# A Mamba and mixture-of-experts block on one core: scan inputs and products over pairs of steps, one table set for Exp and Ln, a wider dt projection, and new orders of the queues

## The chip, the cores and the metric

The kernel runs on 1 core of a Trainium2 chip, in float32 but for small helpers. The metric is the device time of one execution in microseconds. Before the change it is 13,945.11 us, the median of 3 runs (13,933.89 to 13,954.32).

## The reference

16 images of 224x224x3 become 196 patch tokens each, and with 128 text tokens they are 16 sequences (B = 16) of L = 324 tokens with 192 channels. They are normalised, pass 16 Mamba layers (NL = 16, inner width I = 384, state N = 16, rank 48), a final norm, and a mixture of 16 experts with a shared expert. The layers, where nearly all the time goes, compute for each sequence:

```python
h = rmsnorm(x, nw)
u, z = split(h @ in_w.T)
u = silu(causal_conv(u, cw, cb))                       # 4 taps
dt_r, Bm, Cm = split(u @ xp_w.T)                       # 48, 16, 16
dt = softplus(dt_r @ dtw.T + dtb)
for t in range(L):                                     # 16 states n for each of 384 channels i
    state = exp(dt[t, i] * A[i, n]) * state + dt[t, i] * u[t, i] * Bm[t, n]
    y[t, i] = sum_n state[i, n] * Cm[t, n]
x = x + ((y + u * D) * silu(z)) @ ow.T
```

## The kernel before

A *unit* is one sequence in one layer; there are UNITS = 256, layer after layer. All the work of the layers is in `run_layers`. Channels lie on partitions, time along the free axis, so one `tensor_tensor_scan` of VectorE runs a whole recurrence: its 972 elements are three blocks of 324 times. The 16 *steps* s of a unit cover 384 channels x 16 states; each step has 128 partitions (32 channels x 4 states) and 3 blocks, and has nothing to do with time. For each step:

- ScalarE makes the decay, three Exp activations of 323 elements (`se_decay`, L646), into one of two buffers in PSUM (`decay[s % 2]`), when the scan two steps before has left it. One column a block stays zero and cuts the recurrence.
- GpSimd makes the input, `dbu` = `dtu_rep` * `b_rep` (`ge_dbu`, L912), into one of DRING = 4 buffers.
- VectorE scans (`ve_scan`, L847) into one of RING = 8 buffers `h`, and multiplies by C in place (`ve_product`, L856), C being in PSUM, where TensorE broadcasts it for four steps at a time (`te_bcast`, L466). The products of steps 3, 7 and 12 are GpSimd's (`ge_product`, L920) with a C in SBUF (`c_rep`).
- TensorE adds up the four states of a channel with the matrix `fold`, two steps in one `te_sum` (L479), in PSUM (`y_ps`); `te_skip` adds u * D.

When all 16 steps are in `y_ps`, VectorE multiplies by silu(z) (`ve_gate`, L864), and TensorE projects back and adds x (`te_out`). The rest of a unit is prepared ahead. In one step function with number u the engines scan unit u and work on p = u + 1 (softplus, z), k = u + 2 (u, convolution, Silu, x projection, dt projection) and j = u + 3 (norm). All of TensorE's projections go through one PSUM bank, `pj`: ScalarE copies each result out before the next may be written, so `te_z` half 1 waits for `se_z` half 0, and so on. dt = max(x, 0) + ln(1 + exp(-|x|)) + a correction of what 1 + e lost in rounding: ScalarE makes the terms, and three DMAs of GpSimd's queue add them into `dt` (L936), which SP's queue stores in DRAM, and loads back replicated for the 128 partitions of each step (`dt_rep`, `dtu_rep`, 486 KB a piece; `b_rep`, `c_rep`, 162 KB).

Each engine's queue is written out by hand in `tensor_step`, `scalar_step`, `vector_step`, `gpsimd_step` and `sync_step`, and runs strictly in its order; semaphores (`reached`, `wait`) tie them. VectorE's order around a unit's start is: product 15 of the unit before, scans 0 and 1, product 0, the gate of the unit before, scan 2. TensorE's is: sum of squares, sum of steps 12 and 13, broadcast 0, z half 0, sum of steps 14 and 15, z half 1, out. ScalarE switches its activation tables four times a unit (L778, L782, L697, L705): to Ln, to Exp, to Silu, to Exp. Three shorter steps (`early`) run before the loop.

## Time and profile before

| | us |
|---|---|
| median of 3 runs | 13,945.11 |
| profiled execution, span from first to last instruction | 13,964.1 |
| VectorE busy | 12,892.4 (92%) |
| GpSimd busy | 12,631.1 (90%) |
| TensorE busy | 12,204.2 (87%) |
| ScalarE busy | 11,365.0 (81%) |

The profile is of an execution of its own; of it the trace gives the span. The embedding and the first norm take the first 200 us, the layers run to about 12,800, the router and the experts after that. Engines: PE is TensorE's matmuls, PEld its weight loads, DVE VectorE, ACT ScalarE, POOL GpSimd, SP the queue that issues most DMAs. An instruction's end may overlap the start of the next on its engine, so the time that one takes of its engine is read from start to start. "[0.48 <-ACT ps L646]" means that the engine stood idle for 0.48 us before, and that the ScalarE instruction of line 646 ended the wait. "x3" means that three instructions in a row are merged in a row.

### The profile page before, as it was taken

The numbers are of one execution on the slowest core, as the hardware profiler recorded it, in microseconds if no ns is written. First come the engines' busy times: TensorE is split into PE (matmuls) and PEld (weight loads), VectorE is DVE, ScalarE is ACT, GpSimd is POOL, SyncE is SP. The second block draws the span as 40 slices with busy tenths as digits, with TensorE's granted clock in tenths as the row PEclk, the third lists the DMA queues.
The fourth block names the chain that finished last, engine by engine and source line by source line (L and its number), as shares of the span: only waits on it lengthen the run. The fifth ranks groups of instructions, "written<-read, shape, count | busy, mean of one in ns | idle before, by whom it ended". The sixth has DMA issues, their size and how long they took to land. (4 is left out here: it accounts for less than half of the span.)

```text
span 13964.1 us, 203073 instructions
## 1 busy us (share of the span) xinstructions
PE 12204.2 (87%) x51466; PEld 6379.1 (46%) x51466; DVE 12892.4 (92%) x8757; ACT 11365.0 (81%) x21744; POOL 12631.1 (90%) x6352
## 2 busy tenths in 40 slices
PE   7888888888888888888888888888888888888898
PEld 4444444444444444444444444444444444444776
DVE  2999999999999999999999999999999999997533
ACT  4888888888888888888888888888888888887111
POOL 2999999999999999999999999999999999996033
PEclk8999999999999999999999999999999999999899
DMA  4555555555555555555555555555555555554122
GB/s 104 156 160 157 156 164 161 166 154 161 157 161 161 162 161 155 162 156 165 160 165 155 159 159 156 166 161 163 155 161 156 163 161 161 161 155 128 36 63 52
DMA packets 825576, 2086.15 MB, mean 149 GB/s; under 512 B 101243, under 2 KB 381308, under 8 KB 825336
## 3 DMA queue, kind: packets, MB, share of 16 engines
q1 hardware_dynamic: 693720, 1684.45, 36.0%
q0 software_dynamic: 130992, 399.73, 15.2%
q14 instruction: 114, 0.93, 0.0%
q10 hardware_dynamic: 720, 0.55, 0.0%
q8 instruction: 30, 0.49, 0.0%
HBM read 1414.20 MB, written 286.41 MB: 122 GB/s over the span
## 5 line engine op out<-in xcount | busy, mean ns | idle before, releaser
L912 POOL TENSOR_TENSOR dbu<-dtu_rep,b_rep 128x972 f32<-128x972 f32 x4096 | 9534.2, 2511 | 137.2 <-DVE h L847 109.5
L847 DVE TENSOR_TENSOR_SCAN h<-ps,dbu 128x972 f32<-128x972 f32 x4096 | 8723.4, 2166 | 207.8 <-ACT ps L646 207.8
L646 ACT ACTIVATE ps<-dt_rep,A_cur 128x323 f32<-128x323 f32 x12288 | 5842.5, 520 | 957.0 <-DVE h L847 950.5
L856 DVE TENSOR_TENSOR h<-h,ps 128x972 f32<-128x972 f32 x3329 | 3731.2, 1146 | 0.2 <-DVE ps L1206 0.2
L479 PE MATMUL ps<-h,fold 128*32 128x486 f32 x16400 | 3567.5, 577 | 90.1 <-DVE h L856 89.4
L920 POOL TENSOR_TENSOR h<-h,c_rep 128x972 f32<-128x972 f32 x769 | 1853.0, 2410 | 0.0
L557 PE MATMUL ps<-u_raw,w_cv 128*128 128x162 f32 (+7 forms) x8256 | 1801.5, 372 | 28.6 <-ACT u_raw L682 1.5
L479 PEld LDWEIGHTS ps<-h,fold 128*32 128x32 f32 x16400 | 784.9, 110 | 1961.1 <-issue 1731.1
L557 PEld LDWEIGHTS ps<-u_raw,w_cv 128*128 128x128 f32 x8256 | 1351.6, 190 | 509.4 <-ACT u_pre L689 159.5
L543 PE MATMUL ps<-x_norm,w_u 96*128 96x324 f32 (+1 forms) x4128 | 987.7, 383 | 65.1 <-ACT u_raw L682 55.9
L466 PE MATMUL ps<-c_rows,sel_c 16*128 16x324 f32 x2048 | 827.8, 484 | 209.1 <-DVE h L856 201.2
L508 PE MATMUL ps<-x_norm,w_z 96*128 96x324 f32 (+1 forms) x4112 | 983.5, 383 | 1.4 <-ACT rstd L715 0.7
L525 PE MATMUL ps<-y_gated,w_o 128*96 128x324 f32 x3084 | 925.9, 436 | 0.0
L543 PEld LDWEIGHTS ps<-x_norm,w_u 96*128 96x128 f32 x4128 | 665.7, 191 | 541.1 <-ACT u_raw L682 277.9
L586 PE MATMUL ps<-xp_rows,w_dt 49*128 49x162 f32 (+1 forms) x2064 | 562.1, 393 | 388.7 <-ACT dt L743 207.8
L577 PE MATMUL ps<-u_act,w_x 128*128 128x324 f32 x1548 | 490.2, 453 | 461.8 <-ACT u_act L697 454.8
L1854 POOL DMA_INDIRECT e_rows<-n_rows,e_ix x96 | 96.3, 1003 | 863.7 <-issue 472.8
L508 PEld LDWEIGHTS ps<-x_norm,w_z 96*128 96x128 f32 x4112 | 661.1, 190 | 447.0 <-issue 179.5
L466 PEld LDWEIGHTS ps<-c_rows,sel_c 16*128 16x128 f32 x2048 | 299.9, 183 | 834.6 <-DVE h L856 629.8
L586 PEld LDWEIGHTS ps<-xp_rows,w_dt 49*128 49x128 f32 x2064 | 321.0, 187 | 788.0 <-ACT dt L743 429.6
L523 PE MATMUL ps<-x_T,ident 96*96 x1028 | 401.9, 473 | 315.8 <-ACT z_pre L670 201.9
L525 PEld LDWEIGHTS ps<-y_gated,w_o 128*96 128x96 f32 x3084 | 504.5, 164 | 337.0
(186 smaller groups left out, 12885.8 us busy)
## 6 DMA issues: line engine op xcount, KB each, us to landing
dt_rep<-dt_rows SPq DMA_DIRECT2D x1028, 486.0 KB, 5.6
dtu_rep<-dtu_rows SPq DMA_DIRECT2D x1028, 486.0 KB, 4.8
b_rep<-b_rows SPq DMA_DIRECT2D x1028, 162.0 KB, 5.2
dt<-exp_x POOLq DMA_DIRECT2D x257, 486.0 KB, 5.1
dt<-dtu POOLq DMA_DIRECT2D x257, 486.0 KB, 4.4
dt<-u_pre POOLq DMA_DIRECT2D x257, 486.0 KB, 4.4
dt_rows<-dt SPq DMA_DIRECT2D x257, 486.0 KB, 2.6
dtu_rows<-dtu SPq DMA_DIRECT2D x257, 486.0 KB, 2.6
```

The source lines that it names most:

```text
L466: pe.matmul(c_ps, sel_c[64:80, q, :], c_rows[par][64:80, :], start=True, stop=True).then_inc(s_cbc, 1)
L479: mm = pe.matmul(y_ps[32 * r:32 * r + 32, half, :], fold[:, :], src[:, half * YW:(half + 1) * YW], start=(m in (0, 1)), stop=(m < 0))
L508: mm = pe.matmul(pj[:, lo:hi], w_z[:, c, it * 128:it * 128 + 128], x_norm[par][:, c, t:t + hi - lo], start=(c == 0), stop=(c == 1))
L525: mm = pe.matmul(pj[0:HC, 0:L], w_o[:, it, half * HC:(half + 1) * HC], y_gated[:, it, :], start=False, stop=(it == IT - 1))
L543: mm = pe.matmul(pj[:, lo:hi], w_u[:, c, it * 128:it * 128 + 128], x_norm[par][:, c, t:t + hi - lo], start=(c == 0), stop=(c == 1))
L557: mm = pe.matmul(pj[:, lo + skip:hi], w_cv[:, it * KC + KC - 1 - back, :], u_raw[:, it * L + t + skip - back:it * L + t + hi - lo - back], ...
L586: mm = pe.matmul(pj[:, lo:hi], w_dt[:, it * 128:it * 128 + 128], xp_rows[0:RB, t:t + hi - lo], start=True, stop=True)
L646: ins = act.activation(decay[s % 2][:, it * L + 1:(it + 1) * L], dt_rep[:, s % NR, it, 1:L], ACT.Exp, scale=A_cur[:, it * N + s:it * N + s ...
L847: dve.tensor_tensor_scan(h[s % RING][:, :, :].rearrange("p i t -> p (i t)"), decay[s % 2], dbu[s % DRING][:, :, :].rearrange("p i t -> p ( ...
L856: dve.tensor_tensor(h[s % RING][:, :, :], h[s % RING][:, :, :], c_ps.unsqueeze(1).broadcast_to([128, IT, L]), ALU.mult).then_inc(s_prod, 1)
L912: pool.tensor_tensor(dbu[s % DRING][:, :, :], dtu_rep[:, r, :, :], b_rep[:, q, :].unsqueeze(1).broadcast_to([128, IT, L]), ALU.mult).then_ ...
L920: pool.tensor_tensor(h[s % RING][:, :, :], h[s % RING][:, :, :], c_rep[:, at, :].unsqueeze(1).broadcast_to([128, IT, L]), ALU.mult).then_i ...
```

## The change

- GpSimd's input is made for two steps in one instruction of 1944 elements (eight a unit). VectorE's products of steps 0 and 1, 4 and 5, 8 and 9, 10 and 11, 14 and 15 are pairs too; those of 2, 6 and 13 stay alone, and 3, 7 and 12 stay GpSimd's. `dbu` and `h` become one tensor each, so that neighbours lie side by side.
- The scans, Exps, products and sums run in lists of their own (`SCANS`, `EXPS`, `PRODUCTS`, `SUMS`), and the counts that others wait for follow these lists.
- Exp and Ln are taken from the set `natural_log_exp_and_others`; table switches stay only around Silu. What Ln gives at one in that set, measured on the chip at the start (`less`), is subtracted by one more pass over exp_x.
- The dt projection contracts all 128 rows of `xp_rows` with a `w_dt` padded by zeros, instead of 49 rows.
- All five queues have a new order. A step now ends in the middle of a unit: with number u it does the second part of unit u's scan and the first part of unit u + 1's (`v[0]`, `v[1]`), the convolution, dt and z of u + 2, the projection to u of u + 3, the norm of u + 4. Four early steps come before the loop. The gate of unit u stands after scans 1 and 0 of unit u + 1 and waits for the last sum of `SUMS`, that of steps 12 and 13.
- The memsets of `h`, `z_act`, `y_gated`, `c_rep`, `c_ps` and `y_ps` before the layers are gone, and the loop's last step needs no tail of products and outs behind it.

The diff, cut to its core (of the old step functions, which the listing above shows, nothing is repeated):

```diff
-MAIN_SET = "exp_and_others"
+MAIN_SET = "natural_log_exp_and_others"
 LOG_SET = "natural_log"
-FREED = 2 + RING + 1 + 1 + 2 + 1 + 1
+SILU_SET = "silu_and_others"
+FREED = 2
+DEEP = 4
+EXPS = (1, 0, 3, 2, 5, 4, 6, 7, 8, 9, 10, 11, 13, 12, 15, 14)
+SCANS = (1, 0, 3, 2, 4, 5, 6, 7, 8, 9, 10, 11, 13, 12, 15, 14)
+INPUTS = (0, 2, 4, 6, 8, 10, 12, 14)
+PRODUCTS = (0, 2, 6, 4, 8, 10, 13, 14)
+POOL_PRODUCTS = (3, 7, 12)
+SUMS = (0, 2, 4, 6, 8, 10, 14, 12)
+ALONE = (2, 3, 6, 7, 12, 13)
+SUMMED = 2
...
+def both(order, u, s):
+    if s < 0:
+        return both(order, u - 1, s + N)
+    return turn(order, u, max(s, s + 1, key=order.index))
...
+def last(order, steps):
+    return max((s for s in order if s in steps), key=order.index)
...
-        w_dt = sb("w_dt", [RB, I])
+        w_dt = sb("w_dt", [XROWS, I])
...
+        def te_sum(pe, u, s):
+            if any(at in PRODUCTS for at in range(s, s + SUMMED)):
+                reached(pe, s_prod, turn(PRODUCTS, u, last(PRODUCTS, range(s, s + SUMMED))))
+            if any(at in POOL_PRODUCTS for at in range(s, s + SUMMED)):
+                reached(pe, s_pprod, turn(POOL_PRODUCTS, u, last(POOL_PRODUCTS, range(s, s + SUMMED))))
+            if s < NR:
+                reached(pe, s_gate, u)
             for half in range(2):
-                for s in (2 * m, 2 * m + 1):
-                    r = s % NR
-                    src = h[s % RING][:, :, :].rearrange("p i t -> p (i t)")
-                    mm = pe.matmul(y_ps[32 * r:32 * r + 32, half, :], fold[:, :], src[:, half * YW:(half + 1) * YW],
-                                   start=(m in (0, 1)), stop=(m < 0))
+                for step in range(s, s + SUMMED):
+                    r = step % NR
+                    mm = pe.matmul(y_ps[32 * r:32 * r + 32, half, :], fold[:, :],
+                                   flat(h, step)[:, half * YW:(half + 1) * YW], start=(s < NR),
+                                   stop=(s == last(SUMS, range(s % NR, N, NR))))
             mm.then_inc(s_sum, 1)
...
-                mm = pe.matmul(pj[:, lo:hi], w_dt[:, it * 128:it * 128 + 128], xp_rows[0:RB, t:t + hi - lo],
+                mm = pe.matmul(pj[:, lo:hi], w_dt[:, it * 128:it * 128 + 128], xp_rows[:, t:t + hi - lo],
...
+        def tensor_step(pe, u, par):
+            v, q, on = pass_of(u, par)
+            freed = bank_before(u)
+            if on[0]:
+                te_sum(pe, v[0], 2)
+            if on[2]:
+                freed = te_conv(pe, v[2], 0, freed)
+            if on[0]:
+                te_skip(pe, v[0], q[0])
+            if on[2]:
+                freed = te_conv(pe, v[2], 1, freed)
+            if on[0]:
+                te_bcast(pe, v[0], q[0], 2)
+                te_sum(pe, v[0], 4)
+            if on[2]:
+                freed = te_xp(pe, v[2], q[2], freed)
+                freed = te_dt(pe, v[2], 0, freed)
+            if on[0]:
+                te_sum(pe, v[0], 6)
+                te_bcast(pe, v[0], q[0], 3)
+            if on[2]:
+                freed = te_dt(pe, v[2], 1, freed)
+            if on[0]:
+                te_sum(pe, v[0], 8)
+            if on[4]:
+                freed = te_ss(pe, v[4], freed)
+            if on[0]:
+                te_sum(pe, v[0], 10)
+            if on[2]:
+                freed = te_z(pe, v[2], q[2], 0, freed)
+            if on[1]:
+                te_bcast(pe, v[1], q[1], 0)
+            if on[0]:
+                te_sum(pe, v[0], 14)
+            if on[2]:
+                freed = te_z(pe, v[2], q[2], 1, freed)
+            if on[0]:
+                te_sum(pe, v[0], 12)
+                freed = te_out(pe, v[0], 0, freed)
+                freed = te_out(pe, v[0], 1, freed)
+            if on[1]:
+                te_bcast(pe, v[1], q[1], 1)
+            if on[3]:
+                freed = te_u(pe, v[3], q[3], 0, freed)
+            if on[1]:
+                te_sum(pe, v[1], 0)
+            if on[3]:
+                freed = te_u(pe, v[3], q[3], 1, freed)
...
+        def se_less(act, p):
+            reached(act, s_one, p + 1)
+            reached(act, s_l, p + 1)
+            act.activation(exp_x[:, :], exp_x[:, :], ACT.Identity, bias=less[:, 0:1]).then_inc(s_less, 1)
...
+        def scalar_step(act, u, par):
+            v, q, on = pass_of(u, par)
+            if on[0]:
+                se_decay(act, v[0], 8)
+            if on[2]:
+                se_ur(act, v[2], 1)
+            if on[4]:
+                se_sq(act, v[4])
+            if on[0]:
+                se_decay(act, v[0], 9)
+            if on[3]:
+                se_weighted_x(act, v[3], q[3])
+            if on[0]:
+                se_decay(act, v[0], 10)
+            if on[2]:
+                se_conv(act, v[2], 0)
+            if on[0]:
+                se_decay(act, v[0], 11)
+            act.preload_act_table_set(SILU_SET)
+            if on[1]:
+                se_silu_z(act, v[1], q[1])
+            if on[2]:
+                se_conv(act, v[2], 1)
+                se_silu_u(act, v[2], q[2])
             act.preload_act_table_set(MAIN_SET)
+            if on[0]:
+                se_decay(act, v[0], 13)
+            if on[2]:
+                se_xp(act, v[2])
+            if on[0]:
+                se_decay(act, v[0], 12)
+            if on[2]:
+                se_dt(act, v[2], 0)
+            if on[0]:
+                se_decay(act, v[0], 15)
+            if on[4]:
+                se_copy_nw(act, v[4])
+            if on[0]:
+                se_decay(act, v[0], 14)
+            if on[2]:
+                se_dt(act, v[2], 1)
+            if on[1]:
+                se_copy_A(act, v[1])
+            if on[2]:
+                se_exp_x(act, v[2])
+            if on[4]:
+                se_log_ss(act, v[4])
+            if on[1]:
+                se_decay(act, v[1], 1)
+            if on[3]:
+                se_copy_cb(act, v[3])
+            if on[2]:
+                se_one_plus(act, v[2])
+            if on[1]:
+                se_decay(act, v[1], 0)
+            if on[2]:
+                se_log(act, v[2])
+                se_z(act, v[2], 0)
+            if on[1]:
+                se_decay(act, v[1], 3)
+                se_decay(act, v[1], 2)
+            if on[4]:
+                se_rstd(act, v[4])
+            if on[2]:
+                se_z(act, v[2], 1)
+                se_c_rows(act, v[2], q[2])
+                se_less(act, v[2])
+            if on[1]:
+                se_decay(act, v[1], 5)
+            if on[0]:
+                se_out(act, v[0], 0)
+            if on[1]:
+                se_decay(act, v[1], 4)
+            if on[0]:
+                se_out(act, v[0], 1)
+            if on[2]:
+                se_lost(act, v[2])
+            if on[1]:
+                se_decay(act, v[1], 6)
+            if on[3]:
+                se_ur(act, v[3], 0)
+            if on[1]:
+                se_decay(act, v[1], 7)
...
         def ve_scan(dve, u, s):
-            reached(dve, s_exp, 16 * u + s + 1)
-            reached(dve, s_dbu, 16 * u + s + 1)
-            if s % 2 == 0:
-                reached(dve, s_sum, 8 * u + s // 2 - 1)
-            dve.tensor_tensor_scan(h[s % RING][:, :, :].rearrange("p i t -> p (i t)"), decay[s % 2],
-                                   dbu[s % DRING][:, :, :].rearrange("p i t -> p (i t)"),
-                                   0.0, ALU.mult, ALU.add).then_inc(s_scan, 1)
+            reached(dve, s_exp, turn(EXPS, u, s))
+            reached(dve, s_dbu, turn(INPUTS, u, s // 2 * 2))
+            reached(dve, s_sum, turn(SUMS, u, s // SUMMED * SUMMED - RING))
+            dve.tensor_tensor_scan(flat(h, s), decay[s % 2], flat(dbu, s), 0.0, ALU.mult, ALU.add).then_inc(s_scan, 1)
         def ve_product(dve, u, s):
-            if s == min(i for i in range(s // 4 * 4, N) if i not in ON_POOL):
-                reached(dve, s_cbc, 4 * u + s // 4 + 1)
-            reached(dve, s_scan, 16 * u + s + 1)
-            dve.tensor_tensor(h[s % RING][:, :, :], h[s % RING][:, :, :],
-                              c_ps.unsqueeze(1).broadcast_to([128, IT, L]), ALU.mult).then_inc(s_prod, 1)
+            reached(dve, s_cbc, 4 * u + s // NR + 1)
+            n = width(s)
+            reached(dve, s_scan, turn(SCANS, u, last(SCANS, range(s, s + n))))
+            mine = slice(SHARED.get(s, 0), n * IT)
+            dve.tensor_tensor(steps(h, s, n)[:, mine, :], steps(h, s, n)[:, mine, :],
+                              each(c_ps, n)[:, mine, :], ALU.mult).then_inc(s_prod, 1)
         def ve_gate(dve, u, par):
-            reached(dve, s_sum, 8 * u + 2)
-            reached(dve, s_za, u)
+            reached(dve, s_sum, turn(SUMS, u, SUMS[-1]))
+            reached(dve, s_skip, u + 1)
+            reached(dve, s_za, u + 1)
             reached(dve, s_out, 2 * u)
             dve.tensor_tensor(y_gated[:, :, :].rearrange("p i t -> p (i t)").rearrange("p (a b) -> p a b", a=2),
                               y_ps, z_act[par][:, :, :].rearrange("p i t -> p (i t)").rearrange("p (a b) -> p a b", a=2),
                               ALU.mult).then_inc(s_gate, 1)
...
+        def vector_step(dve, u, par):
+            v, q, on = pass_of(u, par)
+            if on[0]:
+                ve_scan(dve, v[0], 7)
+                ve_product(dve, v[0], 6)
+                ve_scan(dve, v[0], 8)
+                ve_scan(dve, v[0], 9)
+                ve_product(dve, v[0], 4)
+                ve_scan(dve, v[0], 10)
+                ve_scan(dve, v[0], 11)
+                ve_product(dve, v[0], 8)
+                ve_product(dve, v[0], 10)
+                ve_scan(dve, v[0], 13)
+                ve_scan(dve, v[0], 12)
+                ve_scan(dve, v[0], 15)
+                ve_scan(dve, v[0], 14)
+                ve_product(dve, v[0], 13)
+                ve_product(dve, v[0], 14)
+            if on[1]:
+                ve_scan(dve, v[1], 1)
+                ve_scan(dve, v[1], 0)
+            if on[0]:
+                ve_gate(dve, v[0], q[0])
+            if on[1]:
+                ve_scan(dve, v[1], 3)
+                ve_scan(dve, v[1], 2)
+                ve_product(dve, v[1], 0)
+                ve_product(dve, v[1], 2)
+                ve_scan(dve, v[1], 4)
+                ve_scan(dve, v[1], 5)
+                ve_scan(dve, v[1], 6)
...
-            reached(pool, s_scan, 16 * u + s + 1 - DRING)
-            pool.tensor_tensor(dbu[s % DRING][:, :, :], dtu_rep[:, r, :, :],
-                               b_rep[:, q, :].unsqueeze(1).broadcast_to([128, IT, L]), ALU.mult).then_inc(s_dbu, 1)
+            reached(pool, s_scan, both(SCANS, u, s - DRING))
+            pool.tensor_tensor(steps(dbu, s, 2), steps(dtu_rep, r, 2), each(b_rep[:, q, :], 2), ALU.mult).then_inc(s_dbu, 1)
...
+        def gpsimd_step(pool, u, par):
+            v, q, on = pass_of(u, par)
+            if on[1]:
+                ge_add(pool, v[1], 2)
+            if on[0]:
+                ge_dbu(pool, v[0], 10)
+            if on[1]:
+                ge_dtu(pool, v[1], q[1])
+            if on[0]:
+                ge_dbu(pool, v[0], 12)
+                ge_product(pool, v[0], 7)
+                ge_dbu(pool, v[0], 14)
+            if on[3]:
+                ge_x_norm(pool, v[3], q[3])
+            if on[0]:
+                ge_product(pool, v[0], 12)
+            if on[1]:
+                ge_dbu(pool, v[1], 0)
+                ge_dbu(pool, v[1], 2)
+                ge_dbu(pool, v[1], 4)
+            if on[2]:
+                ge_add(pool, v[2], 0)
+            if on[1]:
+                ge_dbu(pool, v[1], 6)
+            if on[2]:
+                ge_add(pool, v[2], 1)
+            if on[1]:
+                ge_product(pool, v[1], 3)
+                ge_dbu(pool, v[1], 8)
...
+        def sync_step(sp, u, par, due=()):
+            v, q, on = pass_of(u, par)
+            if "u" in due:
+                reload_u(sp, u + 2)
+            if on[1]:
+                sp_store_dt(sp, v[1])
+            if "d" in due:
+                reload_d(sp, u + 0)
+            if on[1]:
+                sp_store_dtu(sp, v[1])
+                sp_load_b(sp, v[1], q[1], 2)
+            if "c" in due:
+                reload_c(sp, u + 2)
+            if on[1]:
+                sp_load_dtu(sp, v[1], 0)
+            if on[0]:
+                sp_load_c(sp, v[0], q[0], 2)
+            if on[1]:
+                sp_load_c(sp, v[1], q[1], 1)
+                sp_load_dtu(sp, v[1], 1)
+                sp_load_b(sp, v[1], q[1], 0)
+                sp_load_dt(sp, v[1], 1)
+                sp_load_c(sp, v[1], q[1], 0)
+                sp_load_dt(sp, v[1], 0)
+            if on[2]:
+                sp_store_b(sp, v[2], q[2])
+            if on[1]:
+                sp_load_dtu(sp, v[1], 2)
+                sp_load_dtu(sp, v[1], 3)
+            if "x" in due:
+                reload_x(sp, u + 2)
+            if on[1]:
+                sp_load_b(sp, v[1], q[1], 3)
+                sp_load_dt(sp, v[1], 2)
+                sp_load_b(sp, v[1], q[1], 1)
+                sp_load_dt(sp, v[1], 3)
+            if "z" in due:
+                reload_z(sp, u + 2)
+            if "o" in due:
+                reload_o(sp, u + 0)
...
```

## Rows read from the trace of the kernel before

**Rows 1.** The page's busy time of an engine, share of the span, instructions
```profile
PE 12204.2 (87%) x51466; PEld 6379.1 (46%) x51466; DVE 12892.4 (92%) x8757; ACT 11365.0 (81%) x21744; POOL 12631.1 (90%) x6352
```

**Rows 2.** Windows: length, busy us of PE PEld DVE ACT POOL, clock, DMA, GB/s
```profile
2000.00:12000.00 10000.00, 8768.31 (x36476) 4349.47 (x36475) 9903.14 (x6147) 8833.62 (x16801) 9897.46 (x4919) 1.00 0.54 160
```

**Rows 3.** Waits, 2000 to 12000 us: who for whom, us in total, times, longest
```profile
DVE h L847 <- ACT ps L646: 96.9, 204, 0.5
POOL dbu L912 <- DVE h L847: 84.4, 204, 0.5
```

**Rows 4.** Timeline of VectorE: start, us from first start to last end, xcount
```profile
5999.54 6.33 DVE L847 TENSOR_TENSOR_SCAN h<-ps,dbu 128x972 f32<-128x972 f32 x3 [0.48 <-ACT ps L646]
6005.79 3.29 DVE L856 TENSOR_TENSOR h<-h,ps 128x972 f32<-128x972 f32 x3
6009.00 4.25 DVE L847 TENSOR_TENSOR_SCAN h<-ps,dbu 128x972 f32<-128x972 f32 x2
...
6014.22 1.16 DVE L864 TENSOR_TENSOR y_gated<-ps,z_act 128x972 f32<-128x972 f32 x1
...
6048.35 6.33 DVE L847 TENSOR_TENSOR_SCAN h<-ps,dbu 128x972 f32<-128x972 f32 x3 [0.48 <-ACT ps L646]
```

**Rows 5.** Groups of VectorE by line: xcount, busy us, mean ns, idle before
```profile
L856 DVE TENSOR_TENSOR h<-h,ps 128x972 f32<-128x972 f32 x3329 | 3731.2, 1146 | 0.2 <-DVE ps L1206 0.2
...
L288 DVE TENSOR_TENSOR x_T<-x_T,ln_rs 96x648 f32<-96x648 f32 x16 | 12.2, 824 | 27.0 <-ACT ln_rs L313 27.0
```

**Rows 6.** Timeline of TensorE around the first quarter of a unit
```profile
6005.39 1.33 PE L569 MATMUL ps<-sq,ones 96*96 96x324 f32 x4
...
6009.14 0.81 PE L466 MATMUL ps<-c_rows,sel_c 16*128 16x324 f32 x2 [0.25 <-DVE h L856]
...
6009.88 1.90 PE L508 MATMUL ps<-x_norm,w_z 96*128 96x324 f32 x8
...
6011.71 1.82 PE L479 MATMUL ps<-h,fold 128*32 128x486 f32 x8
...
6013.47 1.91 PE L508 MATMUL ps<-x_norm,w_z 96*128 96x162 f32 x8
```

**Rows 7.** Timeline, first unit and last gate of the layers
```profile
295.81 4.25 DVE L847 TENSOR_TENSOR_SCAN h<-ps,dbu 128x972 f32<-128x972 f32 x2 [86.26 <-ACT ps L646]
...
301.69 1.82 PE L479 MATMUL ps<-h,fold 128*32 128x486 f32 x8
...
303.75 1.17 DVE L864 TENSOR_TENSOR y_gated<-ps,z_act 128x972 f32<-128x972 f32 x1 [2.62 <-PE ps L479]
...
12796.14 1.17 DVE L864 TENSOR_TENSOR y_gated<-ps,z_act 128x972 f32<-128x972 f32 x1 [2.83 <-PE ps L479]
```

**Rows 8.** Timeline of ScalarE, end of one unit and start of the next
```profile
6003.14 0.55 ACT L742 ACTIVATE exp_x<-ps 128x486 f32<-128x486 f32 x1
...
6004.18 1.01 ACT L749 ACTIVATE exp_x<-exp_x 128x972 f32<-128x972 f32 x1
...
6005.10 2.79 ACT L646 ACTIVATE ps<-dt_rep,A_cur 128x323 f32<-128x323 f32 x6
...
6007.91 1.28 ACT L778 ACT_TABLE_LOAD   x1
...
6009.21 0.53 ACT L715 ACTIVATE rstd<-ps,eps 96x324 f32<-96x324 f32 x1
...
6009.64 1.09 ACT L753 ACTIVATE dtu<-exp_x,one 128x972 f32<-128x972 f32 x1
```

**Rows 9.** Timeline of GpSimd, second half of the same unit
```profile
6030.14 1.84 POOL L926 TENSOR_TENSOR x_norm<-x_norm,rstd 96x648 f32<-96x648 f32 x1
6031.66 4.71 POOL L912 TENSOR_TENSOR dbu<-dtu_rep,b_rep 128x972 f32<-128x972 f32 x2
...
6040.48 9.07 POOL L912 TENSOR_TENSOR dbu<-dtu_rep,b_rep 128x972 f32<-128x972 f32 x4
```

**Rows 10.** Group of VectorE by line: the memsets ahead of the layers
```profile
L1204 DVE MEMSET h<- 128x972 f32 x8 | 6.9, 868 | 1.3 <-issue 1.3
```

More of the change, by code:

```diff
@@ L527, in te_out, with te_u @@
             mm.then_inc(s_out, 1)
-        def te_u(pe, k, par, half, scan, b1):
+            return s_oev, 2 * u + half + 1
+        def te_u(pe, k, par, half, freed):
+            te_free(pe, freed)
             if half == 0:
@@ new lines, in ge_product, with ge_add @@
+            pool.tensor_tensor(steps(h, s, n)[:, mine, :], steps(h, s, n)[:, mine, :],
+                               each(c_rep[:, at, :], n)[:, mine, :], ALU.mult).then_inc(s_pprod, 1)
+        def ge_add(pool, p, step):
+            term, ready = ((exp_x, s_less), (dtu, s_l), (u_pre, s_lost))[step]
+            reached(pool, ready, p + 1)
+            if step == 0:
+                reached(pool, s_dtev, 2 * p + 2)
+            wait(pool, s_acc, 16 * (3 * p + step))
+            pool.sem_inc(s_held, 1)
+            pool.dma_start(dt[:, :], term[:, :], accum_op=ALU.add).then_inc(s_acc, 16)
@@ L1094, in early @@
         def early(step, eng):
-            step(eng, -3, 1, scan=False, a1=False, b1=False)
-            step(eng, -2, 0, scan=False, b1=False)
-            step(eng, -1, 1, scan=False)
+            for u in range(-DEEP, 0):
+                step(eng, u, u % 2)
         def all_units(step, eng):
             early(step, eng)
-            with eng.Fori(0, UNITS // 2) as pair:
+            with eng.Fori(0, UNITS // 2) as two:
                 for par in range(2):
-                    step(eng, 2 * pair + par, par)
+                    step(eng, 2 * two + par, par)
```

652 lines of the change are left out of this document (205 added, 447 removed).

## The prediction

> **What bounds the kernel now.** I read the page's busy shares first: VectorE is busy for 92% of the span and GpSimd for 90% [rows 1]. Since a share is an average over stages, the windows come next. In the stretch from 2000 to 12000 us, which is nothing but the 16 Mamba layers, VectorE is busy 9903 us of 10000 and GpSimd 9897, TensorE 8768, ScalarE 8834, and the granted clock is 1.00 [rows 2]. So two engines stand at 99%. The waits say what is left: VectorE waits 204 times for a decay of ScalarE, 0.5 us each, and GpSimd 204 times for a scan [rows 3]. That is once a unit, since 10000 us hold 205 units. The timeline shows the same: the group of scans 13 to 15 starts at 5999.54 and again at 6048.35, so a unit takes 48.81 us, with one hole of 0.48 us before that scan [rows 4]. 256 units of 48.81 are 12,495 us, and the trace has 12,500 between the first scan at 295.81 and the last gate at 12796.14 [rows 7]. Nothing else matters much; the whole change lies in this stage.
>
> **VectorE's work.** Ends overlap the next start, so I count from start to start. Three products take 6009.00 - 6005.79 = 3.21 us, 1.07 each; two scans and one product 14.22 - 9.00 = 5.22, so a scan is 2.08; three scans take 6.25, the same [rows 4]. The gate is about 1.08 (its 1.16 less the overlap of 0.08 that a product of 1.14 shows). Now: 16 x 2.085 + 13 x 1.067 + 1.08 = 48.3, plus 0.48 of hole, 48.8, as seen.
> A product over two steps has 1944 elements. From 648 elements (824 ns) to 972 (1146 ns) 324 elements cost 322 ns [rows 5], so 972 more cost 0.97 us, and a pair 1.07 + 0.97 = 2.04; were no fixed part saved it would be 2.13. I take 2.08, in the middle. Five pairs (0, 4, 8, 10, 14) and three single products (2, 6, 13) then cost 13.6 instead of 13.9: VectorE's work becomes 48.0 us a unit (47.8 to 48.3).
>
> **GpSimd.** Four inputs in a row span 9.07 us and one lasts 2.5, so one each 2.19; x_norm with 648 elements goes start to start in 1.52 [rows 9]. 324 elements thus cost 0.67 and the fixed part is some 0.2 us. Eight pairs for 16 singles save 8 x 0.2 = 1.4 (0 if nothing fixed is saved): from 48.3 of work [rows 2] to about 46.9. GpSimd stops being an equal bound. A pair lasts some 4.2 us (4.5 to its visible end) and has two of the four slots of dbu; laid along VectorE's order the tightest places are the pair of steps 0 and 1 (ready 0.4 us before scan 1) and that of 8 and 9 (ready 0.2 to 0.4 us before scan 8). Without the saving they would be late by some 0.4 us; I keep up to 0.4 a unit, 100 us in all, for the upper end.
>
> **ScalarE.** A unit has two table loads fewer (four now, 1.28 us each [rows 8]) and one pass over 972 elements more, about 1.0. That gives back 1.6 us of an engine with 5.7 us of idle time a unit, and brings in what stood behind the hole: scan 13 now has its decay early. In the new order scans 8 to 15 find their decays ready: after the Silu block's second load decay 13 starts about 14.4 us into the step (counted from the start of scan 7), 1.9 us before it is needed. So the 0.48 us go. As to the price of a load: in the trace the next activation starts at 6009.21, 1.30 us after the load at 6007.91 [rows 8].
> The Trainium skill, "ScalarE: Activation LUTs", section "What ACT_TABLE_LOAD costs", puts a switch of sets at about 2.66 us with a drain of 1.38 us. By that rule the two loads left around the Silu block would make decay 13 late by 2 x 1.36 - 1.9 = 0.9 us, a result of its own, which stands as the third rival below; the trace doesn't agree, since Ln starts 0.02 us after the load's end, and the measurement goes first.
>
> **dt projection and queues.** The contraction over 128 rows instead of 49 has the same columns; I cost it at nothing (below nothing too: no saving either), covered by TensorE's 12% of idle time; the larger w_dt is loaded once a layer. In SP's new order each load is issued one to two microseconds or more ahead of its need. The chain from the last add to dt_rep and dtu_rep has some 15 us between its stores and the first decay. If a dtu_rep load for pair 0 came late, scan 1 would be late, and up to 2 us of that would be hidden by what follows.
>
> **The added wait: the gate.** This decides. Now VectorE runs product 15, scans 0 and 1, product 0 and then the gate, so TensorE has 2 x 2.08 + 1.07 = 5.2 us after product 15, and has to do a broadcast, half of z and one sum. In the new order VectorE runs product 14 (of steps 14 and 15), scans 1 and 0, then the gate: 4.17 us. The gate waits for the sums in their order up to that of steps 12 and 13, the last. In TensorE's queue behind the product stand te_bcast(0), te_sum(14), te_z half 1, te_sum(12): the broadcast waits for that product, so all four come after it. Start to start the trace has broadcast 0.74 (9.14 to 9.88), z half 0 1.83 (9.88 to 11.71), sum to z 1.76 (11.71 to 13.47), and a sum lasts 1.82 to its end [rows 6]. z half 1 has the same eight matmuls, 1.83. Sum: 0.74 + 1.76 + 1.83 + 1.82 = 6.15. Before it stand 0.07 us till the product's end is seen and 0.06 for TensorE's start; after it 0.05 to 0.24: at 301.69 a sum starts, and the gate, which waits for it, starts at 303.75, 0.24 us past its end [rows 7]. So 6.3 to 6.5 us against 4.17: VectorE stands still 2.2 to 2.35 us before every gate, **2.25 us**.
> Nothing takes it back. Scans 3 and 2, two products, scans 4 to 6 follow the gate in order, and the next product 14 is 43.9 us of VectorE's work after it, so unit = 48.03 + 2.25 = **50.28 us**. The new slack goes to GpSimd, ScalarE and SP, who need none.
> ScalarE has a say in it: z half 1 also waits for the copy of half 0. From the start of decay 14, 0.1 us after scan 12: decay 1.4, the two halves of dt with the copy of A 1.04, the sum of squares on TensorE 1.33 and 0.4 for its log [rows 6, 8], decay 1, 1 + e, decay 0, Ln and the copy: about 1.4 + 0.15 + 1.05 + 1.4 + 1.0 + 0.56. It ends 9.7 us after scan 12's end; TensorE gets to z half 1 at 7.3 + 0.13 + 2.5 = 9.9. A tie within 0.2 us: later activations would lengthen each unit one for one.
>
> **Sum.** 256 x (50.28 - 48.81) = 256 x 1.47 = +376 us. At the ends: ten or so memsets of 0.87 us that the start waited for go [rows 10], -10; the last step runs also the first third of a unit 256 that nobody needs (scans to step 6, GpSimd's pair 8), some 21 us after the last gate where the old tail took 7, +14; the first gate's wait +2. Together +382 us. The profiled execution's span was 13,964.1; its counterpart would be 14,346. The median of the runs, 13,945.1, lies 19 us under the span, and I carry the difference over: 13,945 + 382, **14,330 us**.
>
> **Rivals.**
> *The gate doesn't hold VectorE (faster).* If TensorE got the two last sums behind each other, with z half 1 before them or beside them, the chain would be 0.13 + 0.74 + 1.76 + 1.82 + 0.1 = 4.55, the stall 0.4, the unit 48.4: -0.4 x 256 + 6, about 13,850 us; with no stall at all 48.03, 13,750. It is faster as soon as the stall is under 0.78 us (48.81 - 48.03), a chain under 4.95. For it: the old trace has sums at other rows of the array overlap (they are short side by side). Against it: queue order puts z half 1 between them, and the two rows where a gate did wait for TensorE show a real wait. Chance 0.08; within 0.2%: 0.03.
> *ScalarE's chain comes first (slower still).* If the copy of z half 0 is 0.5 us later than TensorE wants it, by a wait for the sum of squares or a log, the unit is 50.8, 14,460 us. For: the tie above. Against: all its terms are from rows, and rounded up. 0.10.
> *The table switches cost more.* If the Silu block with its two loads took 2.8 us longer than the loads' rows say, decay 13 would be 0.9 us late, the unit 51.2, 14,560 us; the row of Ln right behind its load speaks against it. If a load stayed between Exp and Ln, both before the copy of z half 0, 2 x 1.3 us a unit, 14,950, which would also be the change not doing what it says. 0.05.
> Forecast as worked out: 0.74, with its own range 14,220 to 14,450 (pair cost 0.2 either way is 50 us, the stall's bounds 25, late inputs 100 up, ends 15).
>
> **How the numbers follow.** Slower: 0.74 + 0.10 + 0.05 = 0.89, of which I give back 0.02 for what I have not seen: 0.87. Within 0.2% (28 us, about what repeated runs of this kernel can tell from no change) 0.04, faster 0.09. The range needs 0.8: the forecast's own, stretched to 14,480 to take in the second case; 14,200 below.
>
> **What would show it.** In the profile after: a wait of the gate for TensorE's ps (the sum's line), 256 times, 2.2 to 2.4 us each, some 570 us in all; no wait of scans for ScalarE; VectorE's busy time lower than before although the span is longer; products in two shapes, the pair at 2.1 us; GpSimd idle 3 us or more a unit; table loads halved. Wrong would be: a gate wait under 0.8 us a unit, scans waiting for dbu, or ps and z_pre waits that shift the copy of z half 0.

## The result, and the profile after

The changed kernel takes 14,542.9 us, the median of 4 runs (14,541.5 to 14,545.0), against 13,948.9 for the kernel before: ratio 1.0428, 95% interval 1.0413 to 1.0443, slower by 594 us. Forecast were 14,330 us and a range of 14,200 to 14,480. The direction and the place were right, the size was not: +382 us forecast, +594 measured.

The page of the kernel after, busy time by engine, beside [rows 1]:

```profile
span 14539.7 us, 197681 instructions
PE 12487.4 (86%) x51486; PEld 6366.1 (44%) x51486; DVE 12822.1 (88%) x7474; ACT 11112.3 (76%) x21526; POOL 12383.5 (85%) x4307
```

VectorE's and GpSimd's busy time went down, by 70 and 248 us, while the span grew by 575.6. So the new time is waiting, not work. Where it is shows in VectorE's groups by form (columns as in [rows 5]):

```profile
L923 DVE TENSOR_TENSOR_SCAN h<-ps,dbu 128x972 f32<-128x972 f32 x4103 | 8655.3, 2159 | 90.4 <-ACT ps L702 90.3
L931 DVE TENSOR_TENSOR h<-h,ps 128x1944 f32<-128x1944 f32 x1281 | 2743.8, 2158 | 0.0
L931 DVE TENSOR_TENSOR h<-h,ps 128x972 f32<-128x972 f32 x769 | 879.2, 1143 | 0.0
L940 DVE TENSOR_TENSOR y_gated<-ps,z_act 128x972 f32<-128x972 f32 x256 | 299.6, 1170 | 777.1 <-PE ps L528 777.1
```

The last field of the last row is the point: 777.1 us of idle time before the gate, all of it ended by TensorE's sums (L528). In the *steady stretch* from 2000 to 12000 us nothing else makes VectorE wait; the waits there, as in [rows 3], are one row:

```profile
DVE y_gated L940 <- PE ps L528: 598.3, 196, 4.1
```

The waits for ScalarE's decay, 96.9 us in that stretch before, are gone. But 598.3 / 196 is 3.05 us a unit where 2.25 were forecast, and the longest is 4.1. The timeline of VectorE over neighbouring units tells why the mean misleads:

```profile
6061.34 1.17 DVE L940 TENSOR_TENSOR y_gated<-ps,z_act 128x972 f32<-128x972 f32 x1 [2.41 <-PE ps L528]
6111.77 1.17 DVE L940 TENSOR_TENSOR y_gated<-ps,z_act 128x972 f32<-128x972 f32 x1 [2.41 <-PE ps L528]
6162.20 1.17 DVE L940 TENSOR_TENSOR y_gated<-ps,z_act 128x972 f32<-128x972 f32 x1 [2.40 <-PE ps L528]
6214.29 1.17 DVE L940 TENSOR_TENSOR y_gated<-ps,z_act 128x972 f32<-128x972 f32 x1 [4.06 <-PE ps L528]
6264.72 1.17 DVE L940 TENSOR_TENSOR y_gated<-ps,z_act 128x972 f32<-128x972 f32 x1 [2.41 <-PE ps L528]
```

There are two kinds of unit. One waits 2.41 us and lasts 50.43 from gate to gate, the other 4.06 and lasts 52.09; of the 196 units of the steady stretch 77 are of the second kind. TensorE's timeline in one of each, first the ordinary:

```profile
5999.60 1.33 PE L608 MATMUL ps<-sq,ones 96*96 96x324 f32 x4 [1.72 <-ACT dt L800]
6000.85 1.82 PE L528 MATMUL ps<-h,fold 128*32 128x486 f32 x8
6002.61 1.91 PE L560 MATMUL ps<-x_norm,w_z 96*128 96x324 f32 x8
6004.45 0.81 PE L515 MATMUL ps<-c_rows,sel_c 16*128 16x324 f32 x2
6005.18 1.82 PE L528 MATMUL ps<-h,fold 128*32 128x486 f32 x8
6006.94 1.91 PE L560 MATMUL ps<-x_norm,w_z 96*128 96x162 f32 x8
6008.78 1.82 PE L528 MATMUL ps<-h,fold 128*32 128x486 f32 x8
```

then the other:

```profile
6201.33 1.33 PE L608 MATMUL ps<-sq,ones 96*96 96x324 f32 x4 [1.75 <-ACT dt L800]
6202.59 3.19 PE L528 MATMUL ps<-h,fold 128*32 128x486 f32 x8
6205.71 2.19 PE L560 MATMUL ps<-x_norm,w_z 96*128 96x324 f32 x8
6207.83 0.81 PE L515 MATMUL ps<-c_rows,sel_c 16*128 16x324 f32 x2
6208.57 1.83 PE L528 MATMUL ps<-h,fold 128*32 128x486 f32 x8
6210.32 1.91 PE L560 MATMUL ps<-x_norm,w_z 96*128 96x162 f32 x8
6212.16 1.82 PE L528 MATMUL ps<-h,fold 128*32 128x486 f32 x8
```

From the broadcast (L515) on the two are alike, and as forecast: 0.73, 1.76, 1.84, 1.82 us. The difference lies before it. The sum of steps 10 and 11 takes 3.12 us to the next start instead of 1.76, and the broadcast starts 6.50 us after the sum of squares instead of 4.85. VectorE's product was done all the while (in that unit scan 1 began at 6205.99), so the gate comes 1.65 us later. The windows of the same stretch (columns as in [rows 2]) show what is different there:

```profile
6200.00:6202.00 2.00, 0.67 (x3) 0.46 (x4) 2.00 (x2) 2.00 (x5) 2.00 (x2) 1.00 0.99 351
6203.00:6206.00 3.00, 3.00 (x9) 0.67 (x6) 3.00 (x3) 3.00 (x7) 3.00 (x2) 0.50 1.02 403
6207.00:6212.00 5.00, 5.00 (x24) 2.47 (x22) 3.23 (x2) 4.62 (x10) 4.35 (x2) 1.00 0.07 28
```

The granted clock is 0.50 from about 6202.9 to 6206.3, the lower of its two levels (1.2 GHz), after a stretch in which TensorE had stood idle for 1.75 us. I call this a *fall*, and a unit without one *undisturbed*. The steady stretch has 77 falls, all at this place, and they are in the 77 long units: each of these is 1.65 us longer, and the other 119 take 50.43 us to a hundredth. In the same stretch of the kernel before there is no fall. The DMA engines, which are full in the slow window (share 1.02), aren't the cause: they are as full at the same place of the ordinary unit, where TensorE issues 16 matmuls in 3 us and not 9:

```profile
6001.30:6004.30 3.00, 3.00 (x16) 1.55 (x12) 3.00 (x3) 3.00 (x8) 2.97 (x2) 1.00 1.02 404
```

The account: from first scan to last gate the layers took 12,500.3 us before [rows 7] and take 13,077.8 now (287.60 to 13365.44), +577.5; all that lies around it, -1.9. An undisturbed unit is 50.43 us, 2.41 of them idle. Of the 777.1 us at the gate 256 x 2.41 = 617 are the fixed chain and 160 the clock.

### The profile page after: what moved, and what is told of

Read it like the earlier page. It is cut to its first block and busy times, and to the rows that moved or that the text cites. A ratio compares the mean times of both kernels' runs of the same rounds, so it can differ in the third digit from the quotient of the medians.

```text
span 14539.7 us, 197681 instructions
## 1 busy us (share of the span) xinstructions
PE 12487.4 (86%) x51486; PEld 6366.1 (44%) x51486; DVE 12822.1 (88%) x7474; ACT 11112.3 (76%) x21526; POOL 12383.5 (85%) x4307
## 5 line engine op out<-in xcount | busy, mean ns | idle before, releaser
L997 POOL TENSOR_TENSOR dbu<-dtu_rep,b_rep 128x1944 f32<-128x1944 f32 x2053 | 9183.0, 4478 | 861.0 <-DVE h L923 827.9
L528 PE MATMUL ps<-h,fold 128*32 128x486 f32 x16392 | 3888.8, 596 | 0.0
L931 DVE TENSOR_TENSOR h<-h,ps 128x1944 f32<-128x1944 f32 (+1 forms) x2050 | 3582.2, 1777 | 0.0
L1006 POOL TENSOR_TENSOR h<-h,c_rep 128x972 f32<-128x972 f32 x769 | 1916.9, 2493 | 0.0
L528 PEld LDWEIGHTS ps<-h,fold 128*32 128x32 f32 x16392 | 793.7, 111 | 2039.8 <-issue 2039.8
L515 PE MATMUL ps<-c_rows,sel_c 16*128 16x324 f32 x2052 | 830.0, 484 | 230.2 <-DVE h L931 230.2
L940 DVE TENSOR_TENSOR y_gated<-ps,z_act 128x972 f32<-128x972 f32 x256 | 299.6, 1170 | 777.1 <-PE ps L528 777.1
L624 PE MATMUL ps<-xp_rows,w_dt 128*128 128x162 f32 (+1 forms) x2064 | 563.0, 395 | 289.1 <-ACT xp_rows L788 286.9
L608 PE MATMUL ps<-sq,ones 96*96 96x324 f32 x1040 | 355.1, 465 | 440.0 <-ACT dt L800 421.0
L1023 POOL TENSOR_TENSOR dtu<-dt,u_act 128x972 f32<-128x972 f32 x257 | 684.3, 2663 | 4.0 <-DMA dt<-u_pre 4.0
L948 POOL TENSOR_TENSOR x_norm<-x_norm,rstd 96x648 f32<-96x648 f32 x259 | 499.9, 1930 | 217.7 <-ACT x_norm L781 217.7
```

The lines of the kernel that those rows point to most:

```text
L515: pe.matmul(c_ps, sel_c[64:80, q, :], c_rows[par][64:80, :], start=True, stop=True).then_inc(s_cbc, 1)
L528: mm = pe.matmul(y_ps[32 * r:32 * r + 32, half, :], fold[:, :], flat(h, step)[:, half * YW:(half + 1) * YW], start=(s < NR), stop=(s == la ...
L931: dve.tensor_tensor(steps(h, s, n)[:, mine, :], steps(h, s, n)[:, mine, :], each(c_ps, n)[:, mine, :], ALU.mult).then_inc(s_prod, 1)
L997: pool.tensor_tensor(steps(dbu, s, 2), steps(dtu_rep, r, 2), each(b_rep[:, q, :], 2), ALU.mult).then_inc(s_dbu, 1)
L1006: pool.tensor_tensor(steps(h, s, n)[:, mine, :], steps(h, s, n)[:, mine, :], each(c_rep[:, at, :], n)[:, mine, :], ALU.mult).then_inc(s_pp ...
L1023: pool.tensor_tensor(dtu[:, :], dt[:, :], u_act[par][:, :, :].rearrange("p i t -> p (i t)"), ALU.mult).then_inc(s_dtu, 1)
```

## The experiments

Each ratio is to the kernel before, run on the same chip, whose median there was between 13,930 and 13,936 us. The changed kernel was measured where the kernel before took 13,948.9, so a difference to it in microseconds has some 19 us in it that belong to the chip. Counts of units are for the steady stretch of the profiled execution; "over 1 us longer" is against that kernel's own undisturbed unit.

**The gate's chain, from TensorE's side.** `te_sum(12)` goes ahead of `te_z` half 1:

```diff
-                freed = te_z(pe, v[2], q[2], 1, freed)
-            if on[0]:
                 te_sum(pe, v[0], 12)
+            if on[2]:
+                freed = te_z(pe, v[2], q[2], 1, freed)
```

> The changed kernel with te_sum(12) ahead of te_z half 1 in TensorE's queue; nothing else moves. Theory (the gate waits for the four TensorE items queued behind product 14): the chain becomes 0.13 + 0.74 (broadcast) + 2.94 (two sums in a row, as the 16 matmuls in one row of the kernel before) + 0.24 = 4.05 us against the 4.17 of scans 1 and 0, so the wait of 2.41 us a unit goes. Where the granted clock dips to 0.5 ahead of the broadcast, some 1.5 us stay; with four dips in ten units 0.6 on the mean. Unit 48.0 to 48.6 instead of 51.0, time 13,780 to 13,930 us. Rival (TensorE is now the bound as a whole, by its lower clock): the wait comes back elsewhere and the time stays above 14,300.

Measured: 13,995.8 us, ratio 1.0037 (1.0023 to 1.0052); 547 us less than the changed kernel. The gate waits no more. Four units in ten take 47.9 us from gate to gate, less than any unit of the kernel before, and in these VectorE never waits. The chain is even shorter than forecast: the two sums, one behind the other in the queue and for different rows of `y_ps`, run side by side, 1.78 us for both in every unit where 2.94 were expected.

```profile
6120.86 1.85 PE L528 MATMUL ps<-h,fold 128*32 128x486 f32 x16
6122.64 1.91 PE L560 MATMUL ps<-x_norm,w_z 96*128 96x162 f32 x8
```

Yet 81 of 203 units are longer by over 1 us, 54 of them at 51.0 to 51.4, and the mean is 49.1. VectorE's waits of the stretch:

```profile
DVE h L924 <- ACT ps L703: 217.8, 170, 2.1
DVE h L924 <- POOL dbu L998: 5.8, 11, 1.2
```

A disturbed unit shows TensorE like this, the first matmuls of the two halves of the out projection, each after an idle stretch, with a window between them:

```profile
6225.06 1.39 PE L571 MATMUL ps<-x_T,ident 96*96 x2 [2.12 <-ACT z_pre L727]
6230.51 1.39 PE L571 MATMUL ps<-x_T,ident 96*96 x2 [0.82 <-ACT x_T L733]
```

```profile
6226.00:6229.00 3.00, 3.00 (x7) 1.42 (x5) 3.00 (x2) 1.82 (x4) 2.69 (x3) 0.50 0.11 21
```

The two halves of the out projection are 5.45 us apart from start to start there, and 3.26 in an undisturbed unit. ScalarE stands in its own queue at their copies, with decay 4 behind the first and decay 6 behind the second, so scans 4 and 6 come 1 and 1.8 us late. So the rival wasn't simply wrong: the gate's wait was the loss, but the lower clock now costs more than before, 246 us of the steady stretch (what its units take over 47.9) against 127 in the changed kernel (over 50.43). The theory's range, 13,780 to 13,930, was missed by 66 us.

**The gate's chain, from VectorE's side.** TensorE's queue as in the changed kernel; `ve_gate` one scan later, after scans 1, 0 and 3:

```diff
+            if on[1]:
+                ve_scan(dve, v[1], 3)
             if on[0]:
                 ve_gate(dve, v[0], q[0])
             if on[1]:
-                ve_scan(dve, v[1], 3)
                 ve_scan(dve, v[1], 2)
```

> The changed kernel with VectorE's gate one scan later (after scans 1, 0 and 3). TensorE's queue is as in the changed kernel. Theory (a fixed chain behind product 14): exactly one scan, 2.08 us, more is covered: gate waits of 0.33 and 1.97 us instead of 2.41 and 4.05, time 14,543 - 533 = 14,010 us. Rival (the out projection, now 2 us later, hands the loss on): a new wait of scans 2 or 4 for ScalarE, and more than 14,200.

Measured: 13,952.8 us, ratio 1.0014 (1.0004 to 1.0024). The waits are the 2.41 less one scan:

```profile
6011.83 1.17 DVE L940 TENSOR_TENSOR y_gated<-ps,z_act 128x972 f32<-128x972 f32 x1 [0.34 <-PE ps L528]
```

Undisturbed units take 48.35 us, 2.08 less, as the theory says, and 49 of 205 are longer by over 1. The time is 57 under the forecast: some 19 of that is the chip, and fewer units have a fall than in the changed kernel. Scans do wait for ScalarE, as the rival has it, but for 34.3 us in the whole stretch. A chain of fixed length behind product 14 is shown from both ends.

**The clock.** In the changed kernel six matmuls by a matrix of zeros are added to `y_ps` in the idle stretch before the sum of squares:

```diff
+            if on[0]:
+                for _ in range(6):
+                    pe.matmul(y_ps[:, 0, 0:128], zero[:, :], ident[:, :], start=False, stop=False)
             if on[4]:
                 freed = te_ss(pe, v[4], freed)
```

> The changed kernel with six matmuls of 128 columns by a matrix of zeros (added to y_ps) in the 1.6 us in which TensorE stands idle before the sum of squares. Theory (the clock falls because TensorE stood idle there): no dips, every gate wait is 2.41 us, unit 50.44 instead of 51.02, time 14,543 - 150 = 14,390 us. Rival (the dips have another cause, or come from the other idle stretches around the out projection): four units in ten keep 4.05, 14,540 us or, by the added work, more.

Measured: 14,389.1 us, ratio 1.0328 (1.0311 to 1.0345). This is the theory's number, but the match to a microsecond is luck: the gain is 154 us by the times and 139 by the ratios (1.0428 against 1.0328, the chip taken out), and the mechanism is not quite the theory's. Of 198 units none is as long as 52.09 any more, and the longest gate wait of the steady stretch is 3.0 us. No fall is left before the gate's chain. In a quarter of the units (51 of 198) the clock falls later instead, in the first part of u's projection, after the idle stretches around the out projection:

```profile
6056.33 0.78 PE L572 MATMUL ps<-x_T,ident 96*96 x2 [1.72 <-issue]
...
6060.15 0.78 PE L572 MATMUL ps<-x_T,ident 96*96 x2 [1.40 <-ACT x_T L736]
...
6066.18 3.31 PE L529 MATMUL ps<-h,fold 128*32 128x486 f32 x8
```

```profile
6066.00:6069.00 3.00, 3.00 (x9) 0.55 (x8) 3.00 (x2) 2.86 (x7) 3.00 (x2) 0.50 0.87 166
```

There it costs 0.4 to 0.6 us a unit instead of 1.65. That idle time before the sum of squares has a part in the falls is shown; that it alone does is refuted. And where a fall lands matters as much as whether there is one.

**The table set alone, in the kernel before.** Both loads around Ln removed, Exp and Ln from one set. What Ln gives at one is not subtracted here, which the changed kernel does with one more pass.

```diff
-MAIN_SET = "exp_and_others"
+MAIN_SET = "natural_log_exp_and_others"
...
-            act.preload_act_table_set(LOG_SET)
             se_log_ss(act, j)
             if b1:
                 se_softplus(act, p, 1)
-            act.preload_act_table_set(MAIN_SET)
```

> The kernel before with one edit: Exp and Ln from one table set, so two loads a unit fewer; Ln's value at one is not taken off, so its output is a little off. Theory (scan 13's hole of 0.48 us is ScalarE's Silu block and what lies before it): ScalarE has 2.6 us more a unit but all of it early in the unit; the hole closes only if the delay is carried from there. ScalarE waits for scans before decays 11 and 12 in the kernel before, so nothing is carried: the hole stays, 13,945 us, within 15. Rival (the prediction's reading, that dropped loads bring in what stood behind the hole): 0.45 a unit, 13,835 us.

Measured: 13,929.4 us against 13,930.2, ratio 1.0000 (0.9990 to 1.0009); the forecast's 13,945 was the level of the other chip. ScalarE is busy 542 us less in the steady stretch and VectorE waits as in [rows 3]:

```profile
DVE h L845 <- ACT ps L646: 97.9, 205, 0.5
```

This part is worth nothing by itself. My price for the hole stands (0.48 us a unit go in the changed kernel), but not the reason that I gave in the prediction: the two loads don't make the hole. What of the new order closes it was not tested; that it is ScalarE's order around the Silu block is my guess.

**The pairs.** In the kernel with the two sums together, first VectorE's products single again, then GpSimd's inputs. The lists are shown; the engine's queue follows them, each single standing where its pair stood.

```diff
-PRODUCTS = (0, 2, 6, 4, 8, 10, 13, 14)
+PRODUCTS = (0, 1, 2, 6, 4, 5, 8, 9, 10, 11, 13, 14, 15)
```

> The kernel with the two sums together, with VectorE's 13 products single again. Forecast of the prediction's term: 0.06 us for each of five pairs, so an undisturbed unit of 47.92 becomes 48.2 (bounds 47.9 and 48.6); the time moves by +75 us if the clock's falls are as frequent. Rival (TensorE's sums start earlier with single products, and that is worth more than the fixed part): unit not longer than 47.9.

Measured: 14,043.4 us, ratio 1.0077 (1.0060 to 1.0093), 48 us more than with pairs, where +75 were forecast for equally frequent falls (here 91 against 105). The undisturbed unit is 48.24 against 47.92, so the forecast of 0.06 us a pair is right.

```diff
-INPUTS = (0, 2, 4, 6, 8, 10, 12, 14)
+INPUTS = tuple(range(16))
```

> The kernel with the two sums together, with GpSimd's 16 inputs single again. Forecast of the prediction's term: 1.3 us more GpSimd work a unit, 48.3 in all, which makes GpSimd the bound: an undisturbed unit of 48.4 instead of 47.9, scans wait for dbu. Rival (singles come out earlier one by one and VectorE never waits, so pairing was worth nothing): unit 47.9.

Measured: 14,139.8 us, ratio 1.0146 (1.0129 to 1.0162), 144 us more; undisturbed unit 48.6, near the 48.4 forecast. GpSimd is busy for 9780 us of 10,000, nearly all the time again, and scans wait for `dbu` 108 times, 47.6 us in all, against 11 times and 5.8 us with pairs. Part of the 144 us is the clock: there are 158 falls, and 100 of 202 units are longer by over 1 us. In the changed kernel, though, every unit has 2.4 us to spare at the gate, and I would not expect the gain of 0.7 to show there; that was not run.

**Keeping the clock.** Again from the kernel with the sums together. The diff is the first of four kernels: ScalarE copies z half 1 ahead of the rstd Exp. The second adds the six zero matmuls before the sum of squares, the third also one zero matmul of 324 columns inside z half 1; the fourth has the six and three of those, but not the earlier copy.

```diff
-            if on[4]:
-                se_rstd(act, v[4])
             if on[2]:
                 se_z(act, v[2], 1)
+            if on[4]:
+                se_rstd(act, v[4])
+            if on[2]:
                 se_c_rows(act, v[2], q[2])
```

> The kernel with the sums together and only the earlier copy of z half 1, no zero matmuls. It tells which of the two edits took the 170 us. Theory A (the idle stretch before the out projection is what starts the falls; the copy did it): 13,850 us. Theory B (the zero matmuls before the sum of squares did it): 13,980 us, a third of the units at 51 as with the sums together alone.

> The kernel with the two sums together, plus two edits against TensorE's idle stretches: ScalarE copies z half 1 ahead of the rstd Exp (idle before the out projection 2.1 us, expected 1.7), and six zero matmuls stand before the sum of squares (idle 1.4 us there, expected near none). Theory (the clock falls after TensorE's idle stretches, and at half clock the out chain costs a unit 3.2 us): fewer units at 51.1 us, most at 47.9; 13,760 us if none is left, 13,850 with one in ten. Rival (the falls don't depend on these stretches): as with the sums together alone, about 13,995.

> The kernel with the sums together, the earlier copy of z half 1 and the six zero matmuls before the sum of squares, plus one zero matmul of 324 columns inside z half 1. Theory (idle stretches of TensorE before the out projection make the clock fall; with about 1.5 us instead of 1.85 there are fewer falls; one more matmul costs no unit time): undisturbed unit 47.9 to 48.0, mean 48.1, 13,790 us. Rival (every added matmul delays the broadcasts and sums enough that units lengthen, as the 48.1 to 48.3 of the filled z): 13,830 us or more.

> The kernel with the two sums together, the six zero matmuls before the sum of squares, and three zero matmuls of 324 columns inside z half 1, which lengthen it by about 1 us in time that it would have waited for ScalarE's copy: idle before the out projection about 1.1 us instead of 2.1. Theory (idle stretches make the clock fall): next to no falls, unit 47.9, 13,760 us. Rival (the falls follow something else, such as how much TensorE does in all): as many as before or more, 13,990 or above.

| kernel | us | ratio (95%) | undisturbed unit | over 1 us longer | falls, us at 0.50 |
|---|---|---|---|---|---|
| sums together | 13,995.8 | 1.0037 (1.0023 to 1.0052) | 47.9 | 81 of 203 | 105, 806 |
| + earlier copy | 13,807.8 | 0.9910 (0.9893 to 0.9926) | 47.9 | 31 of 207 | 81, 382 |
| + copy, six zero matmuls | 13,826.1 | 0.9922 (0.9906 to 0.9939) | 47.9 | 29 of 207 | 60, 280 |
| + copy, six, one in z | **13,770.3** | **0.9885 (0.9869 to 0.9902)** | 47.9 | 13 of 208 | 19, 72 |
| + six, three in z, late copy | 13,836.4 | 0.9926 (0.9910 to 0.9943) | 48.1 to 48.3 | 13 of 206 | 11, 51 |

The last column counts the falls of the steady stretch in the trace's record of the clock, and the time for which they last.

The copy, moved by one activation of 0.46 us, is worth 188 us: the time goes with theory A. The six zero matmuls before the sum of squares add nothing to it in time (13,826 against 13,808), though there are fewer falls. But theory A's reason, less idle time, is not shown by the copy alone. TensorE's waits before the two halves of the out projection, first with the sums together, then with the copy:

```profile
PE ps L571 <- ACT z_pre L727: 451.8, 204, 3.2
PE ps L571 <- ACT x_T L733: 169.2, 204, 0.9
```

```profile
PE ps L571 <- ACT z_pre L727: 400.0, 207, 3.2
PE ps L571 <- ACT x_T L733: 219.6, 207, 1.2
```

The first wait is shorter, in a typical unit 1.78 us instead of 2.12, the second longer by as much, and the sum is 621.0 against 619.6. The falls are only a quarter fewer, but they are shorter: with the sums together 54 units have about 10 us at half clock and are 3.2 us longer, with the copy 7 units. Why they end sooner is open. The zero matmul inside z half 1 does take idle time away, and most falls with it (60 become 19). The first wait is 1.2 us in a typical unit of the best kernel, and in all

```profile
PE ps L575 <- ACT z_pre L734: 278.2, 208, 2.5
```

The share of units over 1 us longer fell from 40% to 15% to 6%. With three zero matmuls (first wait 0.8 us) there are fewest falls, but z half 1 ends too late and every unit pays 0.2 to 0.4 us. The best kernel beats both: 162 us under the kernel before, 773 under the changed one.

## Why the prediction was wrong

*What bounds the kernel, VectorE's work:* right. The pair was taken at 2.08 us from start to start and is (two in 4.16); the unit's work was taken at 48.03 us and is 47.92, the unit of the sums together in which VectorE never waits; [rows 4] had 48.33.

*GpSimd:* right in the main. A pair lasts 4.48 us as forecast, and no scan waits for an input in the steady stretch. Its late inputs, kept for the upper end, never came. The fixed part was taken too large: a pair goes start to start in 4.27 us and two singles in 2 x 2.21, so it is 0.15 us and not 0.2, and eight pairs save 1.2 us (8 x 0.2 would have been 1.6, not the 1.4 that the prediction writes). Nothing in the forecast hung on it.

*ScalarE, the loads:* the hole goes, but not because of the loads, as the table set alone shows. Nor did scan 13 wait for its decay in the steady stretch, as it would have by the third rival. The drain that the Trainium skill ("ScalarE: Activation LUTs", "What ACT_TABLE_LOAD costs") adds to a load is not seen in this case: in both kernels a load starts 0.02 us after the instruction before it ends, and the next starts at most 0.06 us after the load's end, in each of over 190 units. The row of Ln that the prediction went by stands for all.

*dt projection and queues:* right. Over 49 rows a 324-column matmul of it took 459 ns, and now, in TensorE's groups by form, over 128 rows:

```profile
L624 PE MATMUL ps<-xp_rows,w_dt 128*128 128x324 f32 x784 | 298.2, 462 | 218.7 <-ACT xp_rows L788 218.7
```

None of VectorE's waits leads to a load in the steady stretch.

*The gate:* the mechanism was right and the decisive one. The chain itself was 6.15 us in the forecast and is 6.15; the gaps around it were a little larger (0.20 us from scan 1's start to the broadcast, 0.30 behind the last sum). So the gate starts 6.65 us after scan 1, where the forecast had 6.42. With VectorE's work a little under the forecast, the undisturbed unit is 50.43 us instead of 50.28, 38 us in all. The tie between ScalarE's copy and TensorE was as forecast too: the copy of half 0 ends at 6006.75 and z half 1 starts at 6006.94.

*The step that failed* is "Before it stand 0.07 us till the product's end is seen and 0.06 for TensorE's start": it takes TensorE to be waiting for product 14, in every unit, at clock 1.00. I never asked when TensorE gets there. The sum of squares starts 4.65 us before scan 1 and TensorE needs 1.25 + 1.76 + 1.84 = 4.85 us from it to the broadcast, so even in an ordinary unit it arrives 0.20 us after scan 1's start, with the product just done: there is no cover at all. And I had read the clock of the kernel before [rows 2] and carried it over to an order with other idle stretches of TensorE. In four units of ten TensorE, at half clock, is 1.65 us late, and all of it goes through to the gate. That is 160 us, and with the 38 it makes up the 200 by which the layers missed the forecast of +378. Without the falls the kernel would have come out near 14,383 (14,543 less 160), inside the range. The rival "ScalarE's chain comes first" names the same place in time but another cause; the trace shows z half 1 starting right behind the sum in both kinds of unit, so the copy of half 0 was never late. None of the rivals had the clock.

*Ends:* forecast +4 (-10 and +14; the first gate's +2 is in the 378), measured -1.9.

## What to carry to other kernels

When an instruction is moved, count what stands ahead of its releaser in the *other* engine's queue, not only what it needs; 6.15 us behind a product against 4.17 us of cover decided this change, and swapping two lines gave nearly all of it back. And where TensorE's work is on the path, look at its idle stretches in the new order as well as at its busy time, and price the chain once at half clock, from the time at which TensorE can really start it. Pairing short instructions pays by the fixed part alone (0.06 us a pair on VectorE, 0.15 on GpSimd), and was seen to pay where the engine was the bound or near it.

## What the runs showed of the hardware

The granted clock fell to 0.50 for 3 to 10 us although TensorE was busy for 86% of the span. Each fall of the steady stretches came within 8 us of an idle stretch of TensorE of at least 1.4 us (1.5 to 1.75 in the changed kernel, 2.1 to 3.2 with the sums together). An idle stretch of the same length passed without a fall in 119 of 196 units of the changed kernel, so it is not a matter of that stretch alone; what else decides is open. In the kernel before TensorE waited 1.8 us once a unit,

```profile
PE ps L577 <- ACT u_act L697: 364.1, 205, 1.8
```

and the clock stayed at 1.00 in the whole steady stretch. How much a fall costs depends on its place: 1.65 us before the gate's chain, 0.4 to 0.6 in u's projection, and up to 3.2 in the out projection, whose copies stand ahead of decays in ScalarE's queue. There it depends on its length too: with the sums together a unit with about 3 us at half clock was 0.5 us longer, one with 7 us 2.1, one with 10 us 3.2.

Two sums of eight matmuls each, 32 columns of weights wide and written to different rows of one PSUM tile, took 1.78 us when they stood side by side in the queue, and one alone takes 1.76 to the next start.
